# Moving the finishing product of the keys and queries, and its transfers, to the following step

## The reference

```python
q, k, v = jnp.split(shift_tokens(x) @ Wqkv, 3, -1)      # 16 heads of 64
q, k = l2norm(q) * qs, l2norm(k) * ksc                  # t / max(norm(t), 1e-12)
q = q * cos * scale + rotate_half(q) * sin * scale
k = k * cos / scale + rotate_half(k) * sin / scale
out = local_attention(q, k, v)                          # softmax over 64 keys for each window
x = out @ Wo + x
x = ffn_layer(shift_tokens(x)) + x
```

## Time and profile before

| | |
|---|---|
| median of three runs | 5493.87 us (5483.84 to 5496.69) |
| the profiled execution | 5499.49 us, its span 5497.7 us |
| busy share of the span | PE 85%, PEld 50%, DVE 67%, ACT 57%, POOL 37% |
| granted TensorE clock, mean | 0.93 |
| row maxima, one to a step | 384 |

### The profile page before, as it was taken

The page is one execution under the profiler, slowest core; times in us unless marked ns, Lnnn a source line. Parts: engine busy times, 40 slices in busy tenths (PEclk is TensorE's granted clock), DMA queues, the critical chain, the costliest instruction groups (busy, mean ns, idle before and its releaser), DMA issues. The chain is left out here.

```text
span 5497.7 us, 160430 instructions
## 1 busy us (share of the span) xinstructions
PE 4684.0 (85%) x63808; PEld 2744.8 (50%) x63808; DVE 3694.6 (67%) x5172; ACT 3155.3 (57%) x9549; POOL 2034.8 (37%) x1438
## 2 busy tenths in 40 slices
PE   7888888777777689989999899988998899999986
PEld 3333333322222356556666566655665566566553
DVE  5666677533333477777777777777777777777773
ACT  4444444323232367766776677666776766666774
POOL 2222222200000255554555455544555455545551
PEclk9999999877777799999999999999999999999997
DMA  1000000000000333344333433334333433343332
GB/s 45 0 0 0 0 0 0 24 0 0 0 0 0 98 87 87 84 97 94 86 86 91 97 85 87 85 92 96 86 88 93 98 84 87 90 97 86 85 85 74
DMA packets 197282, 340.10 MB, mean 62 GB/s; under 512 B 63568, under 2 KB 63568, under 8 KB 195024
## 3 DMA queue, kind: packets, MB, share of 16 engines
q1 hardware_dynamic: 196560, 330.14, 25.5%
HBM read 34.19 MB, written 6.29 MB: 7 GB/s over the span
## 5 line engine op out<-in xcount | busy, mean ns | idle before, releaser
L377 ACT ACTIVATE c_Pb<-c_S,c_nb 128x64 f32<-128x64 f32 x3072 | 918.0, 325 | 853.6 <-DVE c_nb L663 853.0
L342 POOL TENSOR_TENSOR c_F<-c_tAB 128x1024 f32<-128x1024 f32 x384 | 906.9, 2362 | 367.3 <-DMA c_QK<-c_F 213.8
L330 POOL TENSOR_TENSOR c_Pb<-c_Pb,c_rs 128x512 f32<-128x512 f32 x384 | 400.4, 1043 | 1426.0 <-DVE c_rs L671 1426.0
L644 DVE SCALAR_TENSOR_TENSOR c_tAB<-c_PA,c_WP,c_base 128x1024 f32<-128x1024 f32 x384 | 492.2, 1282 | 306.2 <-PE c_PA L450 305.9
L377 ACT ACTIVATION_READ_ACCUMULATOR c_Pb<-c_S,c_nb 128x1 f32 x3072 | 666.3, 217 | 0.0
L644 DVE SCALAR_TENSOR_TENSOR c_tAB<-c_PB,c_WP,c_base 128x1024 f32<-128x1024 f32 x384 | 491.6, 1280 | 58.8 <-PE c_PB L450 57.1
L334 POOL TENSOR_TENSOR c_sq<-c_sq 128x512 f32<-128x512 f32 x384 | 501.6, 1306 | 3.3 <-issue 2.4
L525 PE MATMUL c_S<-c_PTs,c_VE 64*64 64x32 f32 x10752 | 430.6, 222 | 62.3 <-DVE c_PTs L677 28.9
L659 DVE COPY c_VO<-c_PB 128x512 f32<-128x512 f32 x384 | 263.9, 687 | 320.4 <-PE c_PB L485 320.1
L651 DVE SCALAR_TENSOR_TENSOR c_F<-c_PD,c_F 128x1024 f32<-128x1024 f32 x384 | 466.6, 1215 | 9.0 <-ACT c_PD L368 8.8
L525 PE MATMUL c_S<-c_PTs,c_VO 64*64 64x32 f32 x13824 | 442.9, 222 | 22.8 <-issue 22.1
(11 more groups left out here) (247 smaller groups left out, 9597.9 us busy)
## 6 DMA issues: line engine op xcount, KB each, us to landing
c_QK<-c_F SPq DMA_DIRECT2D x3072, 64.0 KB, 2.0
c_VE<-c_VO SPq DMA_DIRECT2D x384, 128.0 KB
c_VE<-c_VO SPq DMA_DIRECT2D x384, 96.0 KB
c_stage<-in_w_heads SPq DMA_DIRECT2D x24, 256.0 KB, 2.9
c_WT<-in_w_tails SPq DMA_DIRECT2D x6, 1024.0 KB, 6.7
a_W<-in_w_level SPq DMA_DIRECT2D x1, 3335.5 KB, 10.7
c_WT<-in_w_tails SPq DMA_DIRECT2D x6, 537.5 KB, 4.3
b_W<-in_w_level SPq DMA_DIRECT2D x1, 3133.0 KB, 10.2
```

Source lines behind the costliest of these rows:

```text
L330: nc.gpsimd.tensor_tensor(p, p, rs[:, n % 2, :].unsqueeze(2).broadcast_to([P, HS, KEYS]), ALU.mult).then_inc(*p_ready.up())
L342: nc.gpsimd.tensor_tensor(F[:, j % 2], tAB[:, j % 2, 0], tAB[:, j % 2, 1], ALU.add).then_inc(*rotated.up())
L377: e = nc.scalar.activation(Pb[:, n % 2, i, :], S[:, n % 2, r, c * KEYS:(c + 1) * KEYS], ACT.Exp, bias=nb[:, n % 2, r * PS + c:r * PS + c + ...
L644: nc.vector.scalar_tensor_tensor(out=tAB[:, kind, half], in0=bank[:, :].unsqueeze(1).broadcast_to([P, 2, SEQ]), scalar=WP[:, 2 * kind + ha ...
```

## The change

`finish` and `permute` work on the job one step older (n-4 in place of n-3), so each job is finished in the following step. On DVE `finish` stands directly behind `row_max` of the next tile and no longer between `products` of PB and `pt_copy`. On SP `permute` stands ahead of `shift_values` in its step. The other engines' programs are the same, and so is the work.

```diff
+        def job_finished(n, now, nxt):
+            return (n - 4) % NS, nxt if n >= 4 else now
...
                 def step(n, now, nxt, prev, new, fresh):
-                    jb, tb = job_before(n, now, nxt)
+                    jf, tf = job_finished(n, now, nxt)
                     v, tv = v_unit(n, now, nxt)
+                    if tf:
+                        permute(jf, tf)
                     if v % 2 and tv:
                         shift_values(v // 4, v % 4 // 2, tv)
-                    if tb:
-                        permute(jb, tb)
...
                     if now:
                         row_max(n, now)
+                    if tf:
+                        finish(jf, tf)
                     if prev and n == 2:
                         residual(prev)
...
                     if tj:
                         products(j, 1, tj)
-                    if tb:
-                        finish(jb, tb)
                     if now:
                         pt_copy(n, now)
```

## The result

The changed kernel takes 5703.51 us (median of four runs, 5690.27 to 5715.4) against 5490.15 for the kernel before on the same chip: a ratio of 1.0388, 95% interval 1.0357 to 1.0419. Its profiled execution took 5715.4 us with a span of 5713.6; the mean granted clock is 0.915 (0.93 before).

What follows compares the result with a forecast made beforehand. PE was taken as the bound, losing most to waits for POOL. Terms sum to 6.6 us a turn; 43 x 6.6 + 5 x 5 = 309 us on 5493.87 gives 5803, said as 5800, range 5690 to 5885.

Steps and rivals of the forecast that it cites:

- The wait that decides: POOL's `rotate` waiting for key and query transfers: to rise from 213.8 to over 800 us.
- The prize: PE's wait for `pt_copy` before the products with the values: at most 117.9 us could go, some 2.5 a turn.
- The lag: Time from SP's first transfer issue to the `rotate` it frees: taken as 7.5 us, range 7.0 to 8.0.
- d0: Length of step 0: the next sequence's shift comes forward by 0 to 1.13 us; 0.3 taken off.
- d1+d2: Steps 1 and 2 together, from row maximum to row maximum: at least 17.0 us for 14.63, +2.4.
- d3: Step 3: step 4's scores wait for the last job's later transfers; 10.6 us for 8.43, +2.2.
- d4+d5: Steps 4 and 5 together: `v_copy`, second projection and probabilities come later; 17.0 us for 16.06, +0.95.
- d6+d7: Step 6 +0.85 us from ScalarE's later reading of sums; step 7 +0.5 from `finish` ahead of the `hidden` product.
- Waits at the sums: PE waiting for POOL's `add_squares` at line 472: about 0.5 to 3 us in steps 1, 2, 3, 5 and 6.
- Faster: Rival: transfers land before POOL needs them and PE's `pt_copy` waits go; 5376 us, chance 0.05.
- Only the scores of step 4: Rival: late `add_squares` is absorbed, leaving losses in steps 3, 4 and 7, 182 us: 5676, chance 0.10.
- The clock: Rival: PE's new waits lower its clock, adding 82 us on top of the forecast: 5880, chance 0.12.

Runs made afterwards that it cites:

- the swap alone: Kernel before, with `finish` put behind `pt_copy` in the same step and nothing else changed: 5598.81 us, ratio 1.0184.
- the run with the shift moved: Kernel before, with the next sequence's two splitting instructions moved from the end of step 0 to behind `v_copy`: 5488.59 us, ratio 0.9999.
- job 7 put back: Changed kernel, with only job 7 finished in step 2 again, as in the kernel before; the other seven jobs stay moved: 5641.16 us, ratio 1.0277.
- the spare products: Changed kernel, with extra PE products ahead of the sums of steps 2 and 3 and the scores of step 4: 5702.15 us, ratio 1.0408.

## Why the prediction was right, and where its numbers were off

**The wait that decides** was named rightly: `rotate` behind the transfers, forecast over 800 us, is 809.0. Halving the transfers takes away 180 of the 213 us, so the lag is shown to be the cause. **The prize** was rightly bounded: 102.7 of the 117.9 us went. In the swap alone most of it went too, and the time rose by 105 us: it does not pay for a later `finish`.

**The lag** was taken as 7.5 us (7.0 to 8.0) and is 6.92 on average over the 313 waits, 6.7 for the transfers issued in step 3. For the old place it was a fair reading: 7.67 on average over the 162 waits there. This is the term that was mis-sized. Of it, the landing behind the last issue stayed as it was (2.34 before, 2.27 after, on average); SP's block of eight issues shrank from a median of 5.84 us to 4.96. In the kernel before 14% of the issues take over 1 us, where the median is 0.59; in the changed one 4%. Taking the lag from the old places of the issues, from the earlier trace rows, was the error; why issues at the new place are rarely delayed was not tried.

By the terms, with the prediction's working as forecast:

| us a turn | forecast | the turn shown, against the earlier trace rows | mean of 30 turns |
|---|---|---|---|
| d0 | -0.3 | -1.79 | -1.78 |
| d1+d2 | +2.4 | +2.32 | +2.61 |
| d3 | +2.2 | +1.30 | +1.06 |
| d4+d5 | +0.95 | 0.00 | +0.55 |
| d6+d7 | +1.35 | +1.11 | +0.81 |
| turn | +6.6 | +2.94 | +3.26 |

- **Step 0**: the largest miss, and a step that failed. The prediction let the shift come forward by up to 1.13 and held that PE's turning would be the next limit. In fact the shift also took 1.11 in place of 2.73 us, because `rotate`, which now waits for transfers, no longer stands in its way: it starts at 3544.07, within the subtraction, and is itself the longer one there, 2.77 for 2.36. But the gain is no gain of its own. d(0)+d(1) is 17.74 after and 17.75 before, and the run with the shift moved shows that PE needs this in any case. What the earlier R(1) does is to start the chain of step 1 by 1.8 us sooner, so that the +2.4 of steps 1 and 2, right as a distance from R(1), cost 0.8 as seen from R(0).
- **Step 3**: R+1.85, the lag and 1.24 for mask and scores. With 6.7 the sum is 9.8; measured 9.80, forecast 10.6 with 7.5. So the sign that d(3) should be near 10.6 failed; the mechanism held, and the lag's size was off by 0.8.
- **Steps 4 and 5**: with the lag of 6.5 the pair is at 16.0, which is what it was before (16.06); the turn shown has 16.06 again. The mean's +0.55 comes with slow stretches of PE's clock that begin in steps 3 and 4, 31 in the changed kernel and 3 before: the pair is 16.19 in the 14 ordinary turns that ran it at full clock (16.17 in the 29 such turns before) and 17.35 in the other 16. The prediction had the +0.95 from the chain and none of it from the clock.
- **Waits at the sums**: forecast in steps 1, 2, 3, 5 and 6; on average 1.9 us in step 2, 1.2 in step 3, 1.9 in step 6, 0.6 in step 5, and 0.2 to 0.3 in step 1.
- **The other turns**: forecast 5 us for each weight-loading turn and 6.6 for all others. Measured 10.6, and 7.7 in the turns with which the loop begins, 3.5 in those of sequence 0. The prediction had no working for them. Half of the transfers removes the surplus of the loop's first turns and more than half of that of the weight-loading ones, and job 7 put back brings the latter from 89.6 to 81.1; so they hang on the lag as well. Another part is the clock behind the new waits: in the weight-loading turns it was granted 0.90 on average for 0.99 before, in those of sequence 1 0.93 for 0.97, and the spare products shorten these turns. What else makes them worse than the ordinary ones stays open.

So the 309 us came from a right chain with a lag 0.6 to 0.8 too long and steps 0 to 2 too dear by 1.3 to 1.6 us. The 30 ordinary turns were forecast at 30 x 6.6 = 198 and cost 98. The 17 others were forecast at 5 x 5 + 12 x 6.6 = 104 and cost 120: there the forecast was too low, by accident only a little, and this brought the total nearer to the forecast than the ordinary turns alone would have.

**The rivals.** *Faster* fell with the lag: 6.9 us is far from 4.2, and with half of the transfers, at 4.1, the change still loses 32 us. *Only the scores of step 4* (5676) came nearest in time, but its mechanism is refuted: the waits at the sums are there, 269.5 us ahead of the loads, and the run with job 7 put back is still 152 us slower than the kernel before. *The clock* is in part right: slow stretches in the network went from 23 to 69. In the ordinary turns it is the smaller part: the 10 that ran at full clock throughout take 74.91 us, against 72.19 for the 22 such turns before, so 2.7 of the 3.3 us are there without it. In the weight-loading turns and those of sequence 1 it is a larger part: with the spare products 5.9 of 10.6 us and 3.1 of 7.7 are gone. As 82 us on top of the forecast it is not shown: with the waits of steps 2 to 4 filled the whole time stayed the same.

## What to carry to other kernels

When a producer is moved later to free its engine, add up the whole way to the buffer it frees: the issue of every transfer one behind the other, the landing, and what is queued behind the instruction that waits. Measure such a lag at the place where it will be, since the same eight issues took 5.84 us in one place and 4.96 in another. And before a shorter step is booked as a gain, look whether another engine is busy throughout that step and the next: then the step boundary moves and the sum stays. And where a run leaves the time as it was, compare the kinds of turns apart before calling a cost absent: an equal time can hide a gain and a loss.

## What the runs showed of the hardware

VectorE's shift and POOL's additions, both between SBUF tiles, exclude each other rather than share. In the rows above, the cast begun at 3530.02 ends at 3531.10, 0.28 behind the end of `rotate` (3530.82), and the subtraction ends at 3532.79, 0.56 behind the end of `add_squares` (3532.23), which in turn ends 1.13 behind the cast's end and takes 1.45 for its usual 1.28. In 47 of 48 turns before, the subtraction ended 0.55 to 0.56 us behind POOL's instruction. Alone, the cast takes 0.42 us and the subtraction 0.69. So the expectation "half speed" was wrong in its picture: each waits the other out and ends about its own time, less some 0.14 us, behind it. The Trainium skill (SBUF — State Buffer, Who interferes with whom) says of VectorE's two-port modes, which a cast can enter, that whoever issues first gets the ports shared with GpSimd for the whole instruction and the other is blocked, and that a VectorE instruction with two SBUF inputs contends with a GpSimd instruction that reads SBUF. The trace agrees, with these 0.28 and 0.56 us. Had this been priced from the row of the shift beside POOL's, the length of step 0 would have come out nearer, though not the sum of steps 0 and 1.

PE's clock, in the two turns of one kernel: behind a wait of 2.43 us it was granted 0.81 of full speed on average over the next step, a mix of 1.2 and 2.4 GHz, and the same 152 products took 8.53 us in place of 7.01.
